# Row fetches by SyncE and ScalarE in place of one indirect gather in 64 and in 32, in a graph network kernel

## The chip, the cores and the metric

The kernel runs on one core of a Trainium2 chip. The metric is the device time of one execution in microseconds (us), the median over several runs. The engines are TensorE (PE, with its weight loads PEld), VectorE (DVE), ScalarE (ACT), GpSimd (POOL) and SyncE (SP), which only issues transfers. A name with q (SPq, ACTq) is the queue of the engine: issues of transfers, register instructions, waits.

## The reference

Four graph layers one after the other on 12,500 nodes of 64 features and 212,500 edges: a graph convolution, a hyperbolic layer, an attention network of three layers, and a relational network of two. The change touches the attention and the second relational layer:

```python
h = (x @ W).reshape(N, H, C)                          # 8 heads of 8
e = leaky_relu(alpha_s[src] + alpha_d[dst], 0.2)      # one logit for each edge and head
m = segment_max(e, dst);  ex = exp(e - m[dst])
out = segment_sum(h[src] * ex / denom[dst], dst)      # three times
# relational layer, twice
seg = dst * R + edge_type                              # R = 65 kinds of edges
mean = segment_sum(x[src], seg) / max(cnt, 1)
out = einsum('nrd,rdk->nk', mean, W_r) + x @ W_root + b
```

What costs most is `h[src]`: for each edge a row of 72 floats (64 features and 8 logit parts) is fetched from a table in DRAM by its node, and in the relational layers a row of 64 floats by node and kind.

## The kernel before

The edges, sorted by target, are cut into tiles of 128, one edge on each partition. Eight tiles (K = 8) are a chunk, and there are 208 chunks (1,664 tiles). An attention layer (`edges_attention`, once for each of three) and a relational layer (`edges_relational`, twice; the second is the last stage of the program, called the last loop here) pass over the 208 chunks once, with all engines in a software pipeline. What an engine does for chunk c stands in a list of steps with a lead: `(messages, 1)` does in turn t the work of chunk t + 1. `rounds` writes the list out for four turns and puts that in a hardware loop, so that buffers of four slots have fixed numbers q; `slotted` does the same with a second list of steps that runs every other turn.

The steps that matter here, with the lines of the profile:

- POOL, L2166 and L3027: for a chunk it waits until slot q of `from_src` is free (`filled` of the chunk four before) and until its row numbers are there (`gather_at`), then issues eight indirect gathers, one for each tile:

```python
def gather(c, q, i):
    pool.wait_ge(filled, free4(c))
    pool.wait_ge(gather_at, ready(c))
    for k in range(K):
        nc.gpsimd.indirect_dma_start(from_src[:, q, k, :], None, g.gat_src[:, :],
            bass.IndirectOffsetOnAxis(ap=src_at[:, q, k:k + 1], axis=0)).then_inc(got[q], 16)
```

- SP in attention: `load_rows` (L2155, lead 4) loads the places of the targets in their window, 256 KB, into one of two buffers once VectorE (`turned`, L2248) and ScalarE (`far_off`, L2212) have read that of two chunks before; `load_masks` (L2146, lead 3) loads two mask rows. In the last loop SP issues nothing until the end.
- DVE in attention: the two scans over 1,024 edges (L2291, L2298), `turned_ones` (L2248, lead 3), `logits` (L2270, lead 2), the first to read a gathered chunk, `messages` (L2281, lead 1), the last to read it and the one that raises `filled`, and eight adds into the sums (L2329). In the last loop: `messages` (L3152), the membership matrix (L3108), eight adds (L3169).
- ACT in attention: `targets` (L2183, lead 6) makes the row numbers for POOL. In the last loop: `fields` (L3042, L3044, lead 4), which waits for `filled` of the chunk four before, and `activate` (L3052), every other turn, whose result TensorE reads a turn later.
- `bases` (L183) loads numbers from SBUF into registers of an engine, up to eight at a time.
- `typed_tables` stands between the third attention layer and the first relational layer. Its TensorE begins with a wait for three weight loads (`pe.wait_ge(w_in, 48)`), then transposes the sums of the attention block by block (L2417), and only later multiplies with these weights (L2916).

## Time and profile before

| | |
|---|---|
| median of 3 runs | 17307.61 us (17297.01 to 17308.78) |
| profiled execution, its own time | 17330.74 us |
| its span | 17329.0 us |
| busy in it: PE, PEld | 12031.7 us, 8971.5 us |
| DVE, ACT, POOL | 12499.8 us, 7380.6 us, 11519.1 us |
| chain that ended last, largest share | POOL in the last loop (L3027), 8% |

Busy time of POOL counts only the part of a gather that the profile shows as running; the step from one gather to the next is longer. No engine is busy through the span, because its stages have different limits; so each stage is read by itself.

### The profile page before, as it was taken

Reading aid. Unit: us, or ns where it says so; the run is one execution under the profiler, and the core shown is the slowest. Engines: PE = TensorE matmul, PEld = TensorE weight load, DVE = VectorE, ACT = ScalarE, POOL = GpSimd, SP = SyncE. Lnnn points to the kernel's source line nnn. Section 1 sums busy time; section 2 is a strip of 40 time slices with the busy share of each in tenths; the row PEclk is TensorE's granted clock in tenths of the full one; section 3 lists DMA queues with packets and bytes.
Section 4 is the critical chain, followed back from the end, with each engine's and each line's share of the span. In section 5 each row is a group of like instructions: output and inputs, shape, how many; then the busy total and the mean of one; then the engine's idle time right before and its main releaser. Section 6 shows DMA issues by size and latency. Waiting matters only on the chain. (4 is left out here: it accounts for less than half of the span.)

```text
span 17329.0 us, 347894 instructions
## 1 busy us (share of the span) xinstructions
PE 12031.7 (69%) x77017; PEld 8971.5 (52%) x77018; DVE 12499.8 (72%) x30848; ACT 7380.6 (43%) x19204; POOL 11519.1 (66%) x11855
## 2 busy tenths in 40 slices
PE   4443338599997577777777777777777888844444
PEld 2222225466665466665666666666546565533333
DVE  7777769777777788887888878888766666634443
ACT  1111129555554566665666656666441222300000
POOL 2777750377775577776777767777307777777777
PEclk7555555677776555555556555655696777755555
DMA  6333344333335222223222232222494666511111
GB/s 235 96 93 94 93 93 123 109 102 103 102 102 90 73 58 58 58 58 73 58 58 58 58 78 58 58 58 58 161 381 126 180 185 178 176 45 26 26 26 32
DMA packets 1329349, 1689.67 MB, mean 98 GB/s; under 512 B 835210, under 2 KB 903562, under 8 KB 1296591
## 3 DMA queue, kind: packets, MB, share of 16 engines
q1 hardware_dynamic: 899089, 875.57, 17.4%
q0 software_dynamic: 412640, 597.16, 15.7%
q10 hardware_dynamic: 17474, 215.22, 3.3%
q8 instruction: 65, 1.06, 0.0%
q14 instruction: 81, 0.66, 0.0%
HBM read 1072.24 MB, written 618.81 MB: 98 GB/s over the span
## 5 line engine op out<-in xcount | busy, mean ns | idle before, releaser
L2166 POOL DMA_INDIRECT gat_from_src<-gat_src_dram,gat_src_at x4992 | 4821.8, 966 | 1680.6 <-issue 1520.8
L3213 PE MATMUL rel_ps_sum<-all_node,rel_msg 128*64 128x128 f32 x6656 | 1413.5, 383 | 1501.4 <-DVEq L3172 1471.3
L3027 POOL DMA_INDIRECT rel_from_src<-typed_dram,rel_src_at x1664 | 1651.1, 992 | 1079.7 <-ACT rel_src_at L3042 596.7
L2387 PE MATMUL gat_ps_sum<-all_node,gat_msg 128*80 128x128 f32 x9984 | 2266.1, 420 | 42.3 <-DVE gat_msg L2281 7.9
L3213 PEld LDWEIGHTS rel_ps_sum<-all_node,rel_msg 128*64 128x64 f32 x6656 | 1133.8, 199 | 1979.2 <-DVEq L3172 1230.3
L1630 POOL DMA_INDIRECT all_node<-hyp_dst_dram,hyp_src_at x1768 | 1724.9, 976 | 603.0 <-issue 513.3
L2387 PEld LDWEIGHTS gat_ps_sum<-all_node,gat_msg 128*80 128x80 f32 x9984 | 2057.5, 252 | 102.3 <-issue 42.7
L3027 POOL DMA_INDIRECT rel_from_src<-typed_next_dram,rel_src_at x1664 | 1593.3, 958 | 566.2 <-issue 493.0
L1094 POOL DMA_INDIRECT bucket_dram<-all_node,order_index x1664 | 1616.0, 971 | 524.3 <-issue 505.8
L2329 DVE TENSOR_TENSOR again_sums_x<-again_sums_x,gat_ps_sum 80x128 f32 x4992 | 1393.1, 279 | 385.4 <-DVE again_sums_x L2329 213.0
L2291 DVE TENSOR_TENSOR_SCAN gat_ps_log<-gat_masks,gat_top,gat_ps_log 8x1024 f32<-8x1024 bf16 x624 | 1461.9, 2343 | 228.3 <-DVE again_sums_x L2329 220.4
L2365 PE MATMUL gat_ps_log<-all_ident,gat_leaky 128*8 128x128 f32 x4992 | 1074.5, 388 | 710.5 <-DVE gat_leaky L2276 710.5
L2198 ACT ACTIVATE gat_off<-all_iota,gat_edge 128x128 bf16<-128x128 bf16 x4992 | 1515.8, 386 | 0.1
L3169 DVE TENSOR_TENSOR again_sums_x<-again_sums_x,rel_ps_sum 64x128 f32 x3328 | 908.5, 273 | 761.8 <-issue 355.8
L2298 DVE TENSOR_TENSOR_SCAN gat_top<-gat_masks,gat_ps_log 8x1024 f32<-8x1024 bf16 x624 | 1419.4, 2275 | 35.0
L2356 PE MATMUL gat_ps_dst<-gats_gat_here,gat_memberT 128*128 x9984 | 1130.1, 197 | 56.4 <-ACT gat_memberT L2218 43.8
L2356 PEld LDWEIGHTS gat_ps_dst<-gats_gat_here,gat_memberT 128*128 128x128 bf16 x9984 | 970.4, 108 | 344.7 <-issue 102.1
L1242 PE MATMUL order_ps_dst<-all_node 128*128 128x64 bf16 x4992 | 300.6, 240 | 1214.0 <-ACT all_node L1121 1156.2
L2228 ACT ACTIVATE gat_shift<-gat_shift 8x1 f32<-8x1 f32 x624 | 126.3, 202 | 2361.2 <-DVE gat_shift L2305 2361.2
L2365 PEld LDWEIGHTS gat_ps_log<-all_ident,gat_leaky 128*8 128x8 f32 x4992 | 510.0, 112 | 1027.9 <-DVE gat_leaky L2276 642.2
L2374 PE MATMUL gat_ps_top<-all_ident,gat_top 8*128 8x8 f32 x4992 | 501.7, 224 | 628.5 <-DVE gat_shift L2305 628.4
L1242 PEld LDWEIGHTS order_ps_dst<-all_node 128*128 128x128 bf16 x4992 | 271.6, 129 | 1258.9 <-issue 920.4
(571 smaller groups left out, 26929.1 us busy)
## 6 DMA issues: line engine op xcount, KB each, us to landing
typed_dram<-typed_res SPq DMA_DIRECT2D x98, 2080.0 KB, 7.2
typed_next_dram<-rel_res ACTq DMA_DIRECT2D x98, 2080.0 KB
gat_relrow<-in_rows_dram SPq DMA_DIRECT2D x624, 256.0 KB
all_node<-gcn_table_dram SPq DMA_DIRECT2D x1664, 48.0 KB
gat_from_src<-gat_src_dram,gat_src_at POOLq DMA_INDIRECT x4992
bucket_dram<-by_dst_zero POOLq DMA_DIRECT2D x48, 1326.0 KB, 6.6
gsum_rec<-bucket_dram SPq DMA_DIRECT2D x221, 288.0 KB, 2.8
all_node<-lo_rows_dram SPq DMA_DIRECT2D x221, 256.0 KB
```

Source lines behind the costliest of these rows:

```text
L1094: nc.gpsimd.indirect_dma_start(g.bucket[:, :], bass.IndirectOffsetOnAxis(ap=index[:, q, k:k + 1], axis=0), rec[:, q, k, :], None).then_inc ...
L1630: nc.gpsimd.indirect_dma_start(from_dst[:, q, k, :], None, g.hyp_dst[:, :], bass.IndirectOffsetOnAxis(ap=src_at[:, q, k:k + 1], axis=0)).t ...
L2166: nc.gpsimd.indirect_dma_start(from_src[:, q, k, :], None, g.gat_src[:, :], bass.IndirectOffsetOnAxis(ap=src_at[:, q, k:k + 1], axis=0)).t ...
L2198: last = nc.scalar.activation(off[:, k, :], g.iota16[:, :], ACT.Abs, scale=-1.0, bias=edge[:, q, REL, k:k + 1])
L2291: v.tensor_tensor_scan(log_flat, masks[:, q, 0, :], log_flat, top[:, 1 - q % 2, CE - 1:CE], ALU.add, ALU.max).then_inc(step_b, 1)
L2298: v.tensor_tensor_scan(top[:, q % 2, ::-1], masks[:, q, 1, ::-1], log_flat[:, ::-1], -BIG, ALU.add, ALU.max).then_inc(step_b, 1)
L2329: v.tensor_tensor(window, window, ps_sum[0:rows, k, :], ALU.add).then_inc(step_c, 1)
L2356: last = nc.tensor.matmul(dst_v[:, k, :], memberT[:, q % 2, w, k, :], own[:, w, :, :].rearrange("p n h -> p (n h)"), start=w == 0, stop=w ...
L2365: last = nc.tensor.transpose(ps_log[0:H, k, :], leaky[:, q % 2, k, :], g.ident[:, :])
L2387: last = nc.tensor.matmul(ps_sum[0:rows, k, :], msg[:, q % 2, k, :], member[:, q, k, :], start=True, stop=True)
L3027: nc.gpsimd.indirect_dma_start(from_src[:, q, k, :], None, table[:, :], bass.IndirectOffsetOnAxis(ap=src_at[:, q, k:k + 1], axis=0)).then_ ...
L3213: last = nc.tensor.matmul(ps_sum[0:D, k, :], msg[:, q % 2, k, :], member[:, q, k, :], start=True, stop=True)
```

## The change

One tile of a group is no longer gathered by POOL: in attention the last tile of every eighth chunk (one in 64), in the last loop the last tile of every fourth chunk (one in 32). Its 128 rows are fetched one by one into a side buffer `side`, each by a transfer of its own whose address is in a register, 16 rows in each turn, and one further transfer (`relay`) copies the side buffer to the slot when that is free. In attention SP issues all 128; in the last loop SP and ACT issue 64 each. The next group's rows wait until the side buffer has been copied. To give each turn of eight its own place, attention runs in a new loop `eights`. The two mask rows of a chunk are loaded by one transfer instead of two. The numbers of the rows are put on one partition when a stage begins (`single`); in the last loop VectorE turns them into integers first (`single_c`), and ScalarE and SyncE wait for that. In `typed_tables` the wait for the weights moves behind the transposes. The core of the diff:

```diff
+PIECE = 16
+GROUP = P // PIECE
+def fetch_piece(nc, eng, engine, rows, table, index, c, at, landed, top):
+    regs = bases(nc, engine, index, c, count=PIECE, per=PIECE, top=top)
+    for e, reg in enumerate(regs):
+        eng.dma_start(rows[at + e:at + e + 1, :], table[ds(reg, 1), :]).then_inc(landed, 16)
...
 # edges_attention, sync
+                sp.dma_start(single[:, :].rearrange("o (c e) -> o c e", e=P), g.src_p[...]).then_inc(single_in, 16)
+                sp.wait_ge(single_in, 16)
+                def relay(c, r, i):
+                    if r == GROUP - 1:
+                        for h in range(2):
+                            sp.wait_ge(side_in[h], 16 * (P // 2) * (i + 1))
+                            alone(sp, mark_s)
+                        sp.wait_ge(filled, free4(c))
+                        alone(sp, mark_s)
+                        sp.dma_start(from_src[:, r % 4, K - 1, :], side[:, :]).then_inc(side_out, 16)
+                def fetch(c, r, i):
+                    if r == 0 and not (isinstance(i, int) and i == 0):
+                        sp.wait_ge(side_out, 16 * i)
+                        alone(sp, mark_s)
+                    fetch_piece(nc, sp, ENG.SP, side, g.gat_src, single, c, r * PIECE, side_in[r // 4], N)
-                    for n, m in enumerate((g.first_mask, g.last_mask)):
-                        sp.dma_start(masks[:, q, n, :], m[ds(c * CE, CE)].partition_broadcast(H)
-                                     ).then_inc(mask_in[q], 16)
+                    sp.dma_start(masks[:, q, :, :], g.masks[:, ds(c * CE, CE)].partition_broadcast(H)).then_inc(mask_in[q], 16)
-                rounds(sp, [(load_rows, 4), (load_masks, 3)])
+                eights(sp, [(load_rows, 4), (load_masks, 3), (relay, 4), (fetch, 5)])
 # edges_attention, gpsimd
-                    for k in range(K):
+                    for k in range(K if r < GROUP - 1 else K - 1):
 # edges_attention, vector
+                    if r == GROUP - 1:
+                        dve.wait_ge(side_out, 16 * (i + 1))
...
 # typed_tables, tensor
-                pe.wait_ge(w_in, 48)
...
                 pe.wait_ge(flips.row_kept, FLIPS)
+                pe.wait_ge(w_in, 48)
...
 # edges_relational, second layer only
+                    for h in range(2):
+                        sp.dma_start(single[h]..., g.tile_rows[:, h * D:(h + 1) * D]...).then_inc(single_in, 16)
                     sp.dma_start(x[:, :, :], g.xs[:, :, :]).then_inc(x_in, 16)
+                    sp.wait_ge(single_c, 2)
+                    rounds(sp, [(relay, 4), (fetch(sp, ENG.SP, 0, mark_s), 5)])
-                    for k in range(K):
+                    for k in range(K if first or q < 3 else K - 1):
-                    slotted(act, [(fields, 4), (activate, None, LAG)])
+                    act.wait_ge(single_c, 2)
+                    slotted(act, [(fields, 4), (fetch(act, ENG.Activation, 1, mark_a), 5), (activate, None, LAG)])
+                    dve.wait_ge(single_in, 32)
+                    for h in range(2):
+                        v.tensor_copy(single[h], single[h].bitcast(F32)).then_inc(single_c, 1)
```

On SP in attention, in the middle of the loop, a turn was three transfers before (the places of the targets, and the two masks):

```order
L2155 ISA
L2155 DMA gat_relrow<-in_rows_dram 128x1024
L2146 DMA gat_masks<-first_mask_dram 8x1024
L2146 DMA gat_masks<-last_mask_dram 8x1024
```

Now the turn with the copy of the side buffer reads as follows, and the last two rows here come 16 times in this and in every other turn (ISA is the address in a register, TENSOR_LOAD the 16 row numbers):

```order
L2218 ISA
L2218 DMA gat_relrow<-in_rows_dram 128x1024
L2209 DMA gat_shared<-masks_dram 8x2x1024
L2192 ISA
L2196 DMA gat_from_src<-gat_side 128x72
L2201 REGISTER_ALU
L210 ISA
L210 TENSOR_LOAD gat_shared
L220 ISA
L220 DMA gat_side<-gat_src_dram 1x72
```

The fetches stand behind the two loads of the next turns, so SP comes to these only when 16 rows have been issued; its loop body goes from 22 such rows to 309, and VectorE's from 180 to 346 (it holds eight turns now).

On ACT in the last loop, in the middle, a turn was the row numbers for POOL, the fields of the edges, and every other turn the activation:

```order
L3040 REGISTER_ALU
L3042 ISA
L3042 ACTIVATE rel_src_at<-again_edges 128x8
L3044 ACTIVATE rel_edge<-again_edges 128x32
L3049 REGISTER_ALU
L3052 ACTIVATE rel_act_x<-rel_ps_node,rel_bias_col 128x128
```

Now it ends the turn before with its last row fetches and the activation, before it comes to the numbers of the next chunk:

```order
L220 ISA
L220 DMA rel_side<-typed_next_dram 1x64
L3147 REGISTER_ALU
L3150 ACTIVATE rel_act_x<-rel_ps_node,rel_bias_col 128x128
L3138 REGISTER_ALU
L3140 ISA
L3140 ACTIVATE rel_src_at<-again_edges 128x8
L3142 ACTIVATE rel_edge<-again_edges 128x32
```

The activation stands behind 16 row fetches of its turn, and the row numbers for POOL behind both.

## Rows read from the trace of the kernel before

**Rows 1.** The page, part 5, costliest groups: busy, mean ns, idle before

```profile
L2166 POOL DMA_INDIRECT gat_from_src<-gat_src_dram,gat_src_at x4992 | 4821.8, 966 | 1680.6 <-issue 1520.8
L3027 POOL DMA_INDIRECT rel_from_src<-typed_next_dram,rel_src_at x1664 | 1593.3, 958 | 566.2 <-issue 493.0
```

**Rows 2.** Timeline of POOL (start, us, idle before): first and last gather of two stages

```profile
5779.27 0.96 POOL L2166 DMA_INDIRECT gat_from_src<-gat_src_dram,gat_src_at  x1 [50.30 <-ACT gat_src_at L2183]
...
7890.28 0.95 POOL L2166 DMA_INDIRECT gat_from_src<-gat_src_dram,gat_src_at  x1 [0.30 <-issue]
...
15196.69 0.95 POOL L3027 DMA_INDIRECT rel_from_src<-typed_next_dram,rel_src_at  x1 [59.25 <-ACT rel_src_at L3042]
...
17296.03 0.95 POOL L3027 DMA_INDIRECT rel_from_src<-typed_next_dram,rel_src_at  x1 [0.30 <-issue]
```

**Rows 3.** Waits of the whole span: total us, times, longest

```profile
DVE gat_leaky L2270 <- DMA gat_from_src<-gat_src_dram,gat_src_at: 316.4, 470, 4.5
```

**Rows 4.** Timeline inside the second attention layer, one turn of SP and VectorE

```profile
9000.76 0.36 SPq L2155 DMA_DIRECT2D gat_relrow<-in_rows_dram  x1
9001.31 0.28 SPq L2146 DMA_DIRECT2D gat_masks<-first_mask_dram  x1
...
9008.72 0.49 DVE L2248 TENSOR_SCALAR gat_memberT<-gat_relrow,all_lane 128x1024 bf16<-128x1024 bf16 x1
...
9010.41 0.36 SPq L2155 DMA_DIRECT2D gat_relrow<-in_rows_dram  x1
```

**Rows 5.** Lines by themselves: instructions of a queue, ns min/median/max

```profile
L876 SPq DMA_DIRECT2D rel_prime<-in_L_gnn_bias x2: 248/254/260, 12973.4 to 12973.7; - x2
L2146 SPq DMA_DIRECT2D gat_masks<-first_mask_dram x624: 276/282/303, 5778.7 to 12300.6; - x156
L3007 SPq DMA_DIRECT2D rel_table_in<-counted_dram x1664: 332/333/1440, 12987.3 to 15116.4; - x185
L2779 SPq DMA_DIRECT2D typed_dram<-typed_res x98: 319/320/1693, 12422.4 to 12965.2; - x98
L3077 ACTq DMA_DIRECT2D typed_next_dram<-rel_res x98: 338/374/390, 13223.4 to 15186.1; - x98
L183 SPq TENSOR_LOAD <-again_base x208: 521/527/2516, 12986.4 to 15112.1; - x104
L183 ACTq TENSOR_LOAD <-all_order_at x196: 272/278/833, 13187.8 to 15185.7; - x196
```

**Rows 6.** Timeline of SP's queue in the first relational layer: eight window loads

```profile
14019.25 3.95 SPq L3007 DMA_DIRECT2D rel_table_in<-counted_dram  x8
```

**Rows 7.** Transfers by line: count, KB each, median us from issue to landing

```profile
gat_kept_dram<-gat_in_res SPq DMA_DIRECT2D x75, 160.0 KB, 2.1
typed_tab<-gat_kept_dram SPq DMA_DIRECT2D x5, 800.0 KB, 8.9
```

**Rows 8.** Timeline at the start of an attention layer

```profile
5777.73 0.86 SPq L2155 DMA_DIRECT2D gat_relrow<-in_rows_dram  x2
...
5801.67 0.69 DVE L2281 TENSOR_TENSOR gat_msg<-gat_from_src,gat_msg 128x512 f32<-128x512 f32 x1 [0.19 <-ACT gat_msg L2224]
```

**Rows 9.** Queue and ACT at the start of the last loop; integer cast on VectorE

```profile
15195.49 0.60 SPq L2994 DMA_DIRECT2D rel_bias_col<-in_L_gnn_res_b  x1
15195.65 0.21 ACT L3042 ACTIVATE rel_src_at<-again_edges 128x8 int32<-128x8 f32 x1 [9.73 <-DVEq L3185]
...
L362 DVE CAST prep_raw<-prep_raw x5: 1026/1027/1028, 64.7 to 69.0; 128x1664 f32<-128x1664 int32 x5
```

**Rows 10.** Timeline at the start of typed_tables

```profile
12363.52 0.35 SPq L2761 DMA_DIRECT2D typed_tab<-gat_kept_dram  x1
...
12382.29 13.59 PE L2417 MATMUL typed_bank<-all_ident,again_sums_x 80*128 80x80 f32 x100 [20.25 <-DMA typed_w<-in_L_gnn_W]
...
12385.80 0.33 DVE L2468 TENSOR_TENSOR typed_ad_own<-typed_tab 128x160 f32<-128x160 f32 x1 [23.44 <-ACT all_node L2425]
```

**Rows 11.** The page, part 3: queues that bring instructions, packets, MB

```profile
q8 instruction: 65, 1.06, 0.0%
q14 instruction: 81, 0.66, 0.0%
```

More of the change, by code:

```diff
@@ L146, in rounds, with eights, turn, in_fours @@
         turn(t, t // 4, t % 4)
+def eights(eng, steps, count=CHUNKS):
+    def turn(t, i, r):
+        for step, lead in steps:
+            if not isinstance(t, int) or 0 <= t + lead < count:
+                step(t + lead, (r + lead) % GROUP, i + (r + lead) // GROUP)
+    for t in range(-max(lead for _, lead in steps), 0):
+        turn(t, t // GROUP, t % GROUP)
+    full = (count - max(lead for _, lead in steps)) // GROUP
+    with eng.Fori(0, full) as i:
+        for r in range(GROUP):
+            turn(i * GROUP + r, i, r)
+    for t in range(GROUP * full, count):
+        turn(t, t // GROUP, t % GROUP)
+def in_fours(*steps):
+    def four(step):
+        return lambda c, r, i: step(c, r % 4, i * (GROUP // 4) + r // 4)
+    return [(four(step), lead) for step, lead in steps]
 def slotted(eng, steps, count=CHUNKS, slots=OWN_TILES):
@@ L328, in _ @@
                 sp.wait_ge(stored, 1)
-                for n, m in enumerate((g.first_mask, g.last_mask)):
+                for n in range(2):
+                    m = g.masks[n]
                     sp.dma_start(m[0:EP].rearrange("(g p e) -> p g e", p=P, e=P), mask[:, n, :, :]).then_inc(loaded, 16)
@@ L2113, in edges_attention @@
         mark_s = ph.sem("mark_s")
-        mask_in, got, rel_in = ([ph.sem(f"{n}{q}") for q in range(4)] for n in ("mask_in", "got", "rel_in"))
+        single_in, side_out = ph.sems("single_in side_out")
+        side_in = ph.sems("side_in0 side_in1")
+        mask_in, rel_in = ([ph.sem(f"{n}{q}") for q in range(4)] for n in ("mask_in", "rel_in"))
+        got = [ph.sem(f"got{r}") for r in range(GROUP)]
         rows = D + 2 * H
@@ L2118, in edges_attention @@
         lane2 = ph.sb("lane2", [P, 1])
-        masks = ph.sb("masks", [H, 4, 2, CE], BF16)
+        shared = ph.sb("shared", [D, 4, 2, CE], BF16)
+        masks = shared[0:H]
+        single = shared[D // 2:D // 2 + 1].rearrange("p q n e -> p (q n e)").bitcast(I32)[:, 0:CHUNKS * PIECE]
+        side = ph.sb("side", [P, D + H])
         from_src = ph.sb("from_src", [P, 4, K, D + H])
@@ L2333, in add @@
                     return step
[L2334 to L2337 removed]
+                eights(dve, [*in_fours((maxima_so_far, 1), (windows, 0), (maxima, 1), (rescale, 0), (shift_by, 1),
+                                       (turned_ones, 3), (add(0), 0), (of_targets, 2), (add(1), 0)),
+                             (logits, 2),
+                             *in_fours((add(2), 0), (leaky_logits, 2), (arguments, 1), (add(3), 0), (add(4), 0), (add(5), 0),
+                                       (tops_of, 1), (messages, 1), (add(6), 0), (add(7), 0))])
             @block.tensor
@@ L2976, in edges_relational @@
         else:
-            out_made, out_kept, stored, x_in = ph.sems("out_made out_kept stored x_in")
+            out_made, out_kept, stored, x_in, single_in, single_c, side_out = ph.sems(
+                "out_made out_kept stored x_in single_in single_c side_out")
+            side_in = [ph.sems(f"side_in{h}0 side_in{h}1") for h in range(2)]
+            halves = ph.sb("halves", [D, CHUNKS // 4 * D], I32)
+            single = [halves[D // 2 * h:D // 2 * h + 1, :] for h in range(2)]
+            side = ph.sb("side", [P, D])
+            top_row = OWN_TILES * P * R - 1
             x = ph.sb("x", [P, NT, D])
@@ L2980, in edges_relational, with fetch, step @@
             full, rest = N // P, N % P
+        def fetch(eng, engine, h, mark):
+            def step(c, q, i):
+                if q == 0 and not (isinstance(i, int) and i == 0):
+                    eng.wait_ge(side_out, 16 * i)
+                    alone(eng, mark)
+                fetch_piece(nc, eng, engine, side, table, single[h], c, h * D + q * PIECE, side_in[h][q // 2], top_row)
+            return step
         def place_of(engine, j, order, top):
@@ L3149, in messages @@
                 def messages(c, q, i):
-                    dve.wait_ge(got[q], 16 * K * (i + 1))
+                    dve.wait_ge(got[q], 16 * (K if first or q < 3 else K - 1) * (i + 1))
+                    if not first and q == 3:
+                        dve.wait_ge(side_out, 16 * (i + 1))
                     dve.wait_ge(summed, half_ready(c, 1) - 4)
```

41 lines of the change are left out of this document (27 added, 14 removed).

## The prediction

> **What bounds the kernel now.** I read the page's costliest groups first. Two lines on POOL hold 6,656 gathers of nearly one length, 966 and 958 ns, and the idle time ahead of them is almost all "issue", that is, POOL waits for nobody [rows 1]. Then POOL's timeline at both ends of a stage. In an attention layer the first gather starts at 5779.27 and the last of 1,664 at 7890.28, so a step is 2111.01 / 1663 = 1.2694 us; in the last loop it is (17296.03 − 15196.69) / 1663 = 1.2624 us [rows 2]. Once started POOL sets the pace of both. The waits say it from the other side: VectorE waited 316.4 us for gathered rows, 0.51 us for each of the 3 × 208 chunks [rows 3]. A chunk takes POOL 8 × 1.2694 = 10.16 us, so VectorE needs at most 9.65 of its own. With a gather in 64 gone the mean chunk is 63/8 × 1.2694 = 10.00 us: POOL stays ahead of VectorE as the bound, with 0.35 us of room. SP, in the same loop, starts a turn at 9000.76 and the next at 9010.41, and between them issues two more transfers by 9001.59 [rows 4]: over 8 us of each turn are free.
>
> **What is removed.** In attention 3 × 26 = 78 gathers, 78 × 1.2694 = 99.0 us. In the last loop 52, 52 × 1.2624 = 65.6 us. In the stage of the tables, TensorE's first transposes started at 12382.29 with a wait that ended on a weight load, and VectorE's first work on the table at 12385.80 behind them; the table itself, issued at 12363.52 for 0.35 [rows 10], lands some 8.9 us later [rows 7], at 12372.8. If only the kept rows and the table are waited for, the chain starts 10 to 13 us earlier; I take 13 less a little, −12.
>
> **What a row fetch costs its queue.** This decides the change. No row of before shows a queue issuing 16 transfers of one run of 256 bytes. Eight window loads took 3.95 us for eight issues of 0.333, so (3.95 − 0.333)/7 = 0.517 from one to the next, 0.184 of it around the issue (address, bookkeeping) [rows 5, 6]. The issue grows with the number of runs: 0.254 for a single small one, 0.282 for 8 mask rows, 0.333 for 128 rows [rows 5]. So a fetch costs x between 0.254 + 0.184 = 0.438 and 0.517; 0.282 + 0.184 = 0.466 is for eight runs, and one run is nearest to the low end. I take 0.45 on SP. ACT's queue is slower for one shape (338 at least against 320, median 374) [rows 5], so 0.018 to 0.054 more: 0.456 to 0.50, taken 0.465. The 16 row numbers come by one register load: 521 to 527 ns for eight against 272 to 278 for one [rows 5] is 36 ns a register, so 0.527 + 8 × 0.036 = 0.81, with what surrounds it about 1.0.
>
> The Trainium skill ("Runtime: NRT & Kernel Launch", section on instruction fetch mechanics) says that a register load costs about 200 ns a register even in bulk. That would be 3.2 us for 16. The 36 ns of this trace speak against it, and the sum does not use it.
>
> **SP in attention.** Per turn: the two loads with their waits 1.15, the fetches 1.0 + 16x. Per eight turns, 8 × 2.15 + 128x, plus the copy of the side buffer: issue 0.35, landing of the last row and of the copy, about 2.1 each by the nearest transfer [rows 7], less what turns over in between, 3.4 with the loop branch. Hence 20.8 to 21.3 + 128x, against POOL's 63 × 1.2694 = 79.97 us. At x = 0.438 it is 77.4, at 0.45 it is 78.9, at 0.459 it is 80, at 0.517 87.5. The gain exists only while SP keeps up. At the start of a layer SP also has to load `single` and to issue 16 fetches before each load of targets' places: in before both went out at 5777.73 and the first messages came at 5801.67 [rows 8], 24 us later. I count 11 us more for VectorE there; POOL, four chunks ahead, needs its first slot back after about 42 us, which leaves 42 − 24 − 11 = 7 us unused. SP must then make good what it lags at 79.97 − 78.9 = 1.1 us per group, 26 times, and does. The forecast for attention is −99 with little lost.
>
> **The last loop.** SP issued nothing there. Its chain for a group of four turns is 8.4 + 64x = 37.2 against POOL's 31 × 1.2624 = 39.13: it fits. ACT's holds the same 64 fetches, and between them the three activations, the wait for the last landing, SP's copy and its landing, because the next rows wait for the copy: 10.1 + 64x. At 0.456 that is 39.3, at 0.465 39.9, at 0.50 42.1. ACT is so the tighter one, and from x = 0.454 sets the pace: 51 groups × (39.9 − 39.13) is 37, less the 11 us that POOL's four slots give once, 26 lost. At the start, ACT made the first row numbers at 15195.65, straight behind VectorE's numbers [rows 9]. Now it first waits for `single_c`: two loads (0.6 each [rows 9] and 2.1 to land [rows 7]), two integer casts of 3,328 numbers, 1027/1664 = 0.617 ns a number [rows 9], 2.05 us each; and SP's and ACT's lead turn with 16 fetches, 8.4, stands before the second. That is 3.3 + 4.1 + 8.4 = 16 to 18, taken 17. The last loop: −65.6 + 17 + 26 = −23; with an ACT chain that just fits, −49.
>
> **Sum.** −99 − 12 − 23 = −134, made against the profiled 17330.74 us, which lies 23 us (0.13%) over the median 17307.61. From the median that is 17174; I put 17180 for small losses at the two kinds of start.
>
> **The rivals.**
> (a) Both queues fit, with nothing lost (x at most 0.455 on both): −99 − 12 − 49 = −160, 17148. For it: the one-run issue of 0.254. Against it: ACT's slower issues.
> (b) ACT only is late: −134, or between −140 and −50 as x on ACT runs from 0.46 to 0.49 (51 × (10.1 + 64 × 0.49 − 39.13) − 11 = 107 lost). This is the forecast.
> (c) The other side: SP's queue becomes the bound of attention. VectorE's `turned_ones` waits for places of targets whose load stands behind 16 fetches, `filled` comes late, and POOL stands. The loss of a layer is 26 × (G − 79.97) + 11 − 7, G = 21.3 + 128x: at x = 0.466 (G = 80.9) 28 us, three layers 84, and with the ACT chain at 0.49 the whole change is −99 − 12 − 65.6 + 17 + 107 + 84, or +31; at 0.48 on SP a layer loses 75 and the change is +170. It decides from about x = 0.466, which is the issue time of a transfer of eight runs and well inside my bounds.
> (d) The longer loops no longer stay in the engine's instruction store. SP's body goes from 22 listed rows to 309, VectorE's from 180 to 346, and in before the queues that bring instructions moved only 65 and 81 packets in 17 ms [rows 11], that is, the loops of before ran without fetching again. If each pass of eight turns now stops for 1.5 us, a wait like the landing of a small transfer, SP's G rises to 80.4 and VectorE loses 0.2 us a turn of its 0.35: 0 to 15 us a layer, total −135 to −90, near (b); with several stops a pass on both engines, 4 us, SP's G is 83 and a layer loses 80: total +105.
> The Trainium skill (same page and section) gives the store as 512 instructions for most engines and says that a branch outside its window stops the engine until the page is fetched. The 309 rows, with the moves between them, are near that size; no stretch of before shows such a stop.
> (e) The register load costs far more than 36 ns a register: at 200, SP has 8 × 2.4 us more a group, G = 98, and the change costs 26 × 18 × 3 = 1,400 us less 99. One row speaks against it and none for it.
>
> **How the numbers follow.** (a) 0.27, (b) with the mild form of (d) 0.37, (c) with the hard form of (d) 0.33, (e) 0.03. About 0.2%, 35 us, is what a measurement of this kernel can tell from no change. Of (c), which begins at zero net gain in attention, a third lies still below −35 and a quarter inside ±35; so faster 0.27 + 0.34 + 0.03 = 0.64, same 0.11, slower 0.25. The likeliest case by itself is 17140 to 17255. The range reaches from 17135, where all goes well, up to 17420, which takes in (c) to x = 0.475 or so, and leaves some 2 in 10 out.
>
> **What the profile after will show.** If right: first to last gather 2111 → about 2080 in each attention layer, VectorE's wait for gathered rows down but not gone, SP's queue nearly full with steps of 0.45 from one row to the next, a register load of about 0.8; in the last loop POOL's first gather unchanged to 8 us later, its span about 2060, with waits of VectorE for the side buffer or of POOL for ACT's row numbers, and TensorE's transposes of the tables some 12 us nearer to the stage's start. (c) shows as VectorE waiting for `gat_relrow`, and POOL idle behind it; (d) as instruction packets in the hundreds and gaps at the loop's end on SP or VectorE. The prediction is wrong if a fetch step is over 0.466 on SP, or if 16-row turns make SP late for the first chunks by more than the 7 us counted.

## The result

| | before | after |
|---|---|---|
| median of 5 runs | 17306.08 us (17296.0 to 17308.78) | 17213.9 us (17208.51 to 17228.21) |
| profiled execution, its span | 17329.0 us | 17206.8 us |

The changed kernel is 0.5% faster: ratio 0.9949, 95% interval 0.9937 to 0.9961, 92 us less. The forecast was 17180 in a range of 17135 to 17420. The two profiled spans differ by 122 us; some 30 of them belong to these two executions, since that of before lies 25 us over its median and that of after 5 below. So the stages are compared in the traces, and the sizes of the whole in the medians.

POOL's timeline after, its first and last gather of the three attention layers and of the last loop (columns as in [rows 2], which they answer to):

```profile
5776.98 0.96 POOL L2230 DMA_INDIRECT gat_from_src<-gat_src_dram,gat_src_at  x1 [50.29 <-ACT gat_src_at L2247]
7854.97 0.95 POOL L2230 DMA_INDIRECT gat_from_src<-gat_src_dram,gat_src_at  x1 [0.30 <-issue]
7966.90 0.96 POOL L2230 DMA_INDIRECT gat_from_src<-gat_src_dram,gat_src_at  x1 [54.78 <-ACT gat_src_at L2247]
10075.16 0.95 POOL L2230 DMA_INDIRECT gat_from_src<-gat_src_dram,gat_src_at  x1 [0.30 <-issue]
10189.57 0.96 POOL L2230 DMA_INDIRECT gat_from_src<-gat_src_dram,gat_src_at  x1 [55.18 <-ACT gat_src_at L2247]
12291.25 0.95 POOL L2230 DMA_INDIRECT gat_from_src<-gat_src_dram,gat_src_at  x1 [0.30 <-issue]
12925.34 0.96 POOL L3125 DMA_INDIRECT rel_from_src<-typed_dram,rel_src_at  x1 [565.47 <-ACT rel_src_at L3140]
15146.09 0.95 POOL L3125 DMA_INDIRECT rel_from_src<-typed_next_dram,rel_src_at  x1 [68.59 <-ACT rel_src_at L3140]
17173.57 0.95 POOL L3125 DMA_INDIRECT rel_from_src<-typed_next_dram,rel_src_at  x1 [0.31 <-issue]
```

The same of before, as far as [rows 2] does not have them:

```profile
7993.80 0.96 POOL L2166 DMA_INDIRECT gat_from_src<-gat_src_dram,gat_src_at  x1 [54.37 <-ACT gat_src_at L2183]
10105.80 0.95 POOL L2166 DMA_INDIRECT gat_from_src<-gat_src_dram,gat_src_at  x1 [0.30 <-issue]
10210.62 0.96 POOL L2166 DMA_INDIRECT gat_from_src<-gat_src_dram,gat_src_at  x1 [55.16 <-ACT gat_src_at L2183]
12976.57 0.96 POOL L3027 DMA_INDIRECT rel_from_src<-typed_dram,rel_src_at  x1 [569.86 <-ACT rel_src_at L3042]
```

The stage of the tables begins with SP's first load of its table, at 12363.52 before [rows 10]; after it is

```profile
12335.92 0.35 SPq L2829 DMA_DIRECT2D typed_tab<-gat_kept_dram  x1
```

From one first gather to the next, with what lies between two stages, the first layer went from 2214.5 to 2189.9 us (−25), the second from 2216.8 to 2222.7 (+6), the third up to the stage of the tables from 2152.9 to 2146.4 (−7), that stage from 613.0 to 589.4 (−24), the first relational layer, which the change does not touch, from 2220.1 to 2220.8 (+1), the last loop to the end of the span from 2132.3 to 2060.7 (−72). The three attention layers so gained 26 us, where 99 were forecast. The first layer's gathers took 2078.0 us, just 26 steps less than 2111.0; the second's took 2108.3, hardly less than its 2112.0 before. Something else than POOL's gathers bounds the second layer and the third.

The waits after, whole span (total us, times, longest):

```profile
POOL gat_from_src L2230 <- DVE gat_msg L2348: 98.1, 151, 2.0
DVE gat_ps_log L2358 <- issue: 242.8, 82, 3.7
DVE gat_memberT L2312 <- DMA gat_relrow<-in_rows_dram: 185.9, 89, 20.3
```

VectorE's wait for gathered rows, 316.4 us before [rows 3], is gone from the list. In its place VectorE waits for the places of the targets, which SP loads, and POOL now waits for VectorE.

SP's queue in the second layer, around the end of a pass of eight turns (start, us, x count):

```profile
8984.04 2.29 SPq L220 DMA_DIRECT2D gat_side<-gat_src_dram  x6
8989.43 0.37 SPq L2218 DMA_DIRECT2D gat_relrow<-in_rows_dram  x1
8991.22 0.29 SPq L2209 DMA_DIRECT2D gat_shared<-masks_dram  x1
8993.03 6.45 SPq L220 DMA_DIRECT2D gat_side<-gat_src_dram  x16
8999.88 0.36 SPq L2218 DMA_DIRECT2D gat_relrow<-in_rows_dram  x1
9000.43 0.29 SPq L2209 DMA_DIRECT2D gat_shared<-masks_dram  x1
...
9070.55 0.37 SPq L2218 DMA_DIRECT2D gat_relrow<-in_rows_dram  x1
9072.57 0.29 SPq L2209 DMA_DIRECT2D gat_shared<-masks_dram  x1
```

Three things are to be seen. Sixteen fetches take 6.45 us, a step of (6.45 − 0.23)/15 = 0.415. Behind the last fetch of a turn in mid-pass the next load comes after 8999.88 − 8999.48 = 0.40 us; behind the last fetch of a pass it comes after 8989.43 − 8986.33 = 3.10. And from that load to the masks it is 1.8 and 2.0 us there, against 0.55 in the next turn. SP's waits for other engines that stand there take 0.02 us each, since what they wait for has come before, and 2.5 of the 3.10 us lie directly behind the branch instruction. This pass of SP is 9070.55 − 8989.43 = 81.1 us (the median of the layer, from branch to branch, is 81.4), POOL's 63 steps are 80.0, and SP never waited for another engine in the layer, only for its own transfers: SP's queue is the bound. VectorE has the same at the restart of its own loop; here its first scan in mid-pass and at a restart:

```profile
8998.90 2.34 DVE L2358 TENSOR_TENSOR_SCAN gat_ps_log<-gat_shared,gat_top,gat_ps_log 8x1024 f32<-8x1024 bf16 x1 [0.23 <-DVE again_sums_x L2396]
...
9060.69 2.34 DVE L2358 TENSOR_TENSOR_SCAN gat_ps_log<-gat_shared,gat_top,gat_ps_log 8x1024 f32<-8x1024 bf16 x1 [3.49 <-issue]
```

SP's shorter gaps have a pattern. Counted in the trace, they come every 128 instructions, in the changed kernel as in e9 below, and take 0.34 to 0.40 us. The first of a pass stands 103 instructions behind the branch in the first layer, 8 in the second and 38 in the third. The one that stands 8 behind takes more, 1.1 us here and 1.3 in the median. It is most of the stop ahead of the masks, and the second layer's pass is the longest of the three (80.1, 81.4 and 80.9 us in the median).

The page's queues that bring instructions, which answer to [rows 11]: q14 went from 81 packets to 890.

```profile
q14 instruction: 890, 7.29, 0.1%
q8 instruction: 65, 1.06, 0.0%
```

Lines by themselves, which answer to [rows 5] (ns min/median/max):

```profile
L220 SPq DMA_DIRECT2D gat_side<-gat_src_dram x9984: 224/228/332, 5778.7 to 12288.2; - x200
L220 ACTq DMA_DIRECT2D rel_side<-typed_next_dram x3328: 227/235/552, 15138.5 to 17138.2; - x196
L210 SPq TENSOR_LOAD <-gat_shared x624: 1132/1147/1307, 5777.3 to 12280.6; - x156
```

The theory that I took from this: SP's own work of a pass is some 77 us and fits under POOL's 80.0, as forecast; a body of 482 instructions (counted in the trace between two branches back) has to be fetched again in each pass, and the stops for that, 2.5 us at the restart and 1.1 to 2.4 in the middle, carry it over. The rivals: VectorE's own restart stop is the bound, or the fetches as such are too much work.

### The profile page after: what moved, and what is told of

It reads as the page before. It is cut to its first block and busy times, and to the rows that moved or that the text cites. A ratio compares the mean times of both kernels' runs of the same rounds, so it can differ in the third digit from the quotient of the medians.

```text
span 17206.8 us, 398106 instructions
## 1 busy us (share of the span) xinstructions
PE 12023.1 (70%) x77017; PEld 8979.5 (52%) x77018; DVE 12471.9 (72%) x30850; ACT 7302.4 (42%) x19204; POOL 11362.2 (66%) x11725
## 3 DMA queue, kind: packets, MB, share of 16 engines
q14 instruction: 890, 7.29, 0.1%
## 5 line engine op out<-in xcount | busy, mean ns | idle before, releaser
L2230 POOL DMA_INDIRECT gat_from_src<-gat_src_dram,gat_src_at x4914 | 4733.0, 963 | 1718.0 <-issue 1459.8
L3125 POOL DMA_INDIRECT rel_from_src<-typed_next_dram,rel_src_at x1612 | 1536.8, 953 | 560.2 <-issue 484.0
L2358 DVE TENSOR_TENSOR_SCAN gat_ps_log<-gat_shared,gat_top,gat_ps_log 8x1024 f32<-8x1024 bf16 x624 | 1461.9, 2343 | 372.0 <-issue 242.8
L2365 DVE TENSOR_TENSOR_SCAN gat_top<-gat_shared,gat_ps_log 8x1024 f32<-8x1024 bf16 x624 | 1419.2, 2274 | 28.0
L2433 PE MATMUL gat_ps_log<-all_ident,gat_leaky 128*8 128x128 f32 x4992 | 1004.8, 369 | 486.8 <-DVE gat_leaky L2343 486.1
L2442 PEld LDWEIGHTS gat_ps_top<-all_ident,gat_top 8*128 8x128 f32 x4992 | 468.5, 176 | 978.2 <-issue 978.2
```

Of the source, the lines that this page charges most:

```text
L2358: v.tensor_tensor_scan(log_flat, masks[:, q, 0, :], log_flat, top[:, 1 - q % 2, CE - 1:CE], ALU.add, ALU.max).then_inc(step_b, 1)
L2365: v.tensor_tensor_scan(top[:, q % 2, ::-1], masks[:, q, 1, ::-1], log_flat[:, ::-1], -BIG, ALU.add, ALU.max).then_inc(step_b, 1)
L2433: last = nc.tensor.transpose(ps_log[0:H, k, :], leaky[:, q % 2, k, :], g.ident[:, :])
L3125: nc.gpsimd.indirect_dma_start(from_src[:, q, k, :], None, table[:, :], bass.IndirectOffsetOnAxis(ap=src_at[:, q, k:k + 1], axis=0)).then_ ...
```

## The experiments

**The parts alone.** e1 keeps the change of attention, e2 that of the last loop, e6 that of the tables' stage; all else is as before.

> The change in attention alone (row fetches by SP, one mask transfer, loops of eight turns); the stage of the tables and the last loop as before. Theory: the layers themselves gave back most of the 99 us, because SP's queue is the bound of the second and third layer (81.3 us for a pass of eight turns against POOL's 80.0). From the trace of the changed kernel, first gather to first gather, the three layers changed by -25, +6 and -20, so -35 to -42 us, ratio 0.9976 to 0.9980. Rival, the one of the prediction: near -99, ratio 0.9943, with the loss somewhere else in the program.

Measured: 17310.81 us against 17321.53, ratio 0.9991 (0.9982 to 1.0), −11 us. Less than my expectation of −35 to −42, and a tenth of the forecast's −99. The interval leaves it at 0 to −31. My expectation had counted the third layer at −20; by the rows above it is −7, so the traces say −26, which the interval holds. The first two layers took 17 us more in e1's trace than in the changed kernel's: SP's passes are longer there by 0.3 and 0.5 us (80.4 and 81.9 in the median). Why its stops differ between the two programs stays open. The rival, −99 with the loss elsewhere, is out: the loss is in attention.

> The change in the last loop alone. Theory: both queues fit, POOL stays the bound, and the start costs some 9 us: -65.6 - 6 + 9, so -55 to -65 us, ratio 0.9962 to 0.9968. Rival (ACT's chain sets the pace, as forecast): -23 to -49 us with spans of POOL over 39.5 us for a group of 31 gathers.

Measured: 17273.0 against 17321.53, ratio 0.997 (0.9958 to 0.9982), −48 us. By the time alone that is in the rival's range, and the interval, −31 to −73, holds the theory's too; the trace tells them apart. In the changed kernel's trace SP copies its side buffer once in four turns. Its first copies, while the queues run ahead of POOL, and two later ones:

```profile
15243.77 0.49 SPq L3109 DMA_DIRECT2D rel_from_src<-rel_side  x1
15280.39 0.48 SPq L3109 DMA_DIRECT2D rel_from_src<-rel_side  x1
15317.41 0.48 SPq L3109 DMA_DIRECT2D rel_from_src<-rel_side  x1
...
16086.37 0.48 SPq L3109 DMA_DIRECT2D rel_from_src<-rel_side  x1
16125.58 0.48 SPq L3109 DMA_DIRECT2D rel_from_src<-rel_side  x1
```

The chain of both queues takes 36.6 to 37.0 us by itself and is later held at POOL's 39. ACT's activations begin only at 15335.71, behind these first three copies, but they change nothing: the next copies, at 15353.53, 15389.99, 15426.35 and 15462.73, are 36.4 us apart. The chain fits. What is lost is the start: POOL's first gather of the loop comes 15146.09 − 15076.55 = 69.5 us behind the last gather of the loop before it (rows further down), against 15196.69 [rows 2] − 15136.49 = 60.2 before. One pair of traces says little here, since this gap varies with nothing changed at it. e3 leaves the last loop as it was and has 48.8:

```profile
15150.72 0.95 POOL L3053 DMA_INDIRECT rel_from_src<-typed_dram,rel_src_at  x1 [0.30 <-issue]
15199.52 0.95 POOL L3053 DMA_INDIRECT rel_from_src<-typed_next_dram,rel_src_at  x1 [47.85 <-ACT rel_src_at L3068]
```

Over all traces the gap is 48.8 to 60.2 us in the four without the change of the last loop (before, e1, e3, e6; mean 54.8) and 67.9 to 76.0 in the six that have it as made (the changed kernel, e2, e4, e5, e7, e9; mean 71.5). The start costs some 17 us, and the gathers of the loop take 67 less, 2094.7 us in the mean of the four and 2027.6 in that of the six: −50 together, which e2's time bears out.

> Only the wait for the weights in the stage of the tables moves behind the transposes. The prediction's step: -12 us, since TensorE's first transpose starts 10.4 us earlier behind the stage's start in the changed kernel; ratio 0.9993. Rival (more is behind it, because last gather of attention to first gather of the relational layer went from 661 us with attention changed alone to 634): -20 to -27 us, ratio 0.9985 to 0.9988. Third: 0, the stage's stores to the table are its bound.

```diff
-                pe.wait_ge(w_in, 48)
...
                 pe.wait_ge(flips.row_kept, FLIPS)
+                pe.wait_ge(w_in, 48)
```

Measured: 17294.37 against 17312.33, ratio 0.999 (0.9981 to 0.9999), −18 us, between −12 and the rival's −20 to −27; its interval, −2 to −33, holds all of these. The parts alone add up to −11 − 48 − 18 = −77, against −92 for the whole, a difference that their intervals hold too. TensorE's timeline of e6, its first transposes:

```profile
12363.19 7.84 PE L2417 MATMUL typed_bank<-all_ident,again_sums_x 80*128 80x80 f32 x64 [1.53 <-PEq L213]
12371.29 5.06 PE L2417 MATMUL typed_bank<-all_ident,again_sums_x 80*128 80x80 f32 x36 [0.25 <-ACT all_node L2425]
```

They begin at 12363.19 instead of 12382.29 [rows 10], 19.1 us earlier, with the start of the stage less than 1 us apart in the two traces: they wait neither for weights nor for the table.

**The length of the loop alone.** e3 is the kernel before with `eights` in place of `rounds` on SP, POOL and VectorE in attention, for example:

```diff
-                rounds(sp, [(load_rows, 4), (load_masks, 3)])
+                eights(sp, in_fours((load_rows, 4), (load_masks, 3)))
```

> The kernel before with loops of eight turns instead of four on SP, POOL and VectorE in attention, and nothing else. SP's body stays near 36 instructions, VectorE's goes from 208 to about 410. Theory (instruction store): VectorE stops 2.6 to 3.0 us at every restart of its loop, SP and POOL do not; VectorE's own turn rises from 9.65 to about 9.97 us, which is still under POOL's 10.16, so the time is that of before within 10 us and VectorE's waits for gathered rows fall from 316 us to about 120. Rival (VectorE's stall alone is what bounds attention in the changed kernel, at 81.3 us a pass): VectorE's waits for gathered rows fall to under 40 us. Second rival (the stall comes from something else than the length of the loop): no stall, waits near 316.

Measured: 17327.03 against 17321.53, ratio 1.0003 (0.9994 to 1.0012): the same. VectorE's body is 405 instructions instead of 208 and stops at every restart, SP's has 91 and does not. The waits of e3:

```profile
DVE gat_ps_log L2317 <- issue: 243.9, 72, 3.5
DVE gat_leaky L2296 <- DMA gat_from_src<-gat_src_dram,gat_src_at: 185.4, 262, 4.5
```

The idle time at a stop is 243.9/72 = 3.4 us and comes from the length alone; it costs nothing that the time shows (the interval is −10 to +21 us) while VectorE has its 0.5 us a turn. Its waits for gathered rows fell from 316 to 185 us, not to 120, so it has more room left than I thought, and at a pass of 80 us it is not the bound. The packets of q14 went from 81 to 452.

**SP with less to do.** e4 fetches rows at fixed addresses:

```diff
-                    fetch_piece(nc, sp, ENG.SP, side, g.gat_src, single, c, r * PIECE, side_in[r // 4], N)
+                    bases(nc, ENG.SP, single, c, count=PIECE, per=PIECE, top=N)
+                    for e in range(PIECE):
+                        row = r * PIECE + e
+                        sp.dma_start(side[row:row + 1, :], g.gat_src[row * 97:row * 97 + 1, :]).then_inc(side_in[r // 4], 16)
...
```

> The changed kernel, but in attention SP fetches rows at addresses fixed in the program instead of the rows that the numbers name (the features of one tile in 64 are so not those of the reference). A fetch is one instruction instead of three, and seven loads of one register in a turn give SP the time back that this saves; so SP has about the same work in a turn, and a body of some 300 instructions instead of 482. Theory (SP bound by the work plus fetches of instructions): the stop at the restart of SP's loop (2.5 us) and those in its middle (0.3 to 1.3) are gone, a pass is POOL's 80.0 us or VectorE's 79.4, and the three layers take 30 to 45 us less than in the changed kernel: 17170 to 17185, ratio 0.9921 to 0.9930. Rivals: SP is bound by the work of the fetches as such, or VectorE's own stall is the bound: no change against the changed kernel, ratio 0.9945 to 0.9952, pass 81.3.

Measured: 17148.87 against 17321.53, ratio 0.9899 (0.9884 to 0.9914), −173 us, past my expectation, and for a reason that spoils the test: its trace holds none of the register loads of the attention layers. Nothing used what they loaded, and so, it seems, they were left out of the program. SP had not the same work but 30 us a pass less, with a body of 212 instructions. What it still shows: VectorE's body is the same 405 instructions with the same stops, and the layers run at 80.0 us a pass. This ends the rival that VectorE's stop is the bound. It says nothing on whether SP's work or its instruction fetches are.

e7 takes one of SP's transfers away instead and leaves its body long (443 instructions): ACT's queue loads the places of the targets.

```diff
+                def load_rows(c, q, i):
+                    act.wait_ge(turned, free2(c))
...
-                eights(sp, [(load_rows, 4), (load_masks, 3), (relay, 4), (fetch, 5)])
+                eights(sp, [(load_masks, 3), (relay, 4), (fetch, 5)])
...
-                rounds(act, [(exponents, 1), (targets, 6), (distances, 2), (fields, 4), (zero_ones, 2), (exp_shift, 2),
+                rounds(act, [(load_rows, 4), (exponents, 1), (targets, 6), (distances, 2), (fields, 4), (zero_ones, 2), (exp_shift, 2),
```

> The changed kernel, but in attention ACT's queue issues the load of the targets' places (256 KB a turn) at the start of its turn, so SP has masks, fetches and the copy. Bodies stay long: SP some 410 instructions, VectorE 405. Theory: SP's pass falls from 81.4 to some 77 us, instruction stops included, and what SP is late with no longer holds VectorE; VectorE at 77 + 2.8 is just inside POOL's 80.0, so the layers are POOL's again: 40 to 75 us less than the changed kernel, 17140 to 17175 by 17306 before, ratio 0.9905 to 0.9925. Rival (VectorE's restart stall bounds the layers): no change against the changed kernel, 0.9945 to 0.9952. Second rival: ACT, which waits 3.8 us a turn for VectorE, becomes late with its far ones, slower than the changed kernel.

Measured: 17140.99 against 17312.33, ratio 0.9903 (0.9888 to 0.9919), −171 us, at the upper end of the gain that the theory gave. POOL's first and last gather of the second layer in e7:

```profile
7970.59 0.96 POOL L2223 DMA_INDIRECT gat_from_src<-gat_src_dram,gat_src_at  x1 [54.73 <-ACT gat_src_at L2247]
10041.94 0.95 POOL L2223 DMA_INDIRECT gat_from_src<-gat_src_dram,gat_src_at  x1 [0.30 <-issue]
```

2071.4 us for 1,638 gathers instead of 2108.3. Both stops at a restart are still there (2.6 us on SP, 2.8 on VectorE in the median), so a stop costs only where its engine has no room.

**The same instructions, fewer restarts.** This is the test of the cause. e9 writes four passes into the body of SP's loop, so that the order and the number of instructions that run stay the same (1,922 in the loop for four passes, against 4 × 482 = 1,928) and one restart in four is left:

```diff
-                eights(sp, [(load_rows, 4), (load_masks, 3), (relay, 4), (fetch, 5)])
+                eights(sp, [(load_rows, 4), (load_masks, 3), (relay, 4), (fetch, 5)], passes=4)
```

> The changed kernel, but SP's loop in attention holds four passes (32 turns, some 1,930 instructions) instead of one: the same instructions in the same order, and a restart only in every fourth pass. Theory (the stop at the restart belongs to the branch back, 2.4 us more than a restart of a short loop): SP's pass falls by 3/4 x 2.4 = 1.8 us where it is the bound, from 81.4 to about 79.6 in the second layer and from 81.0 to 79.2 in the third, so POOL takes over at 80.0: 1.4 + 1.0 us a pass, 25 passes each, 55 to 65 us with the shorter tails less than the changed kernel at best, at least 30; ratio 0.991 to 0.993. Rival 1 (fetching the code itself costs, wherever it is needed: the stops in the middle of the body, 0.3 to 1.3 us, come as often or grow): the pass stays at 81 us or more, ratio 0.9945 or higher. Rival 2 (SP bound by the work of its fetches): no change either, with the stop at the restart gone.

Measured: 17157.06 against 17316.57, ratio 0.9909 (0.9892 to 0.9925), −160 us: 67 more than the change as it was made, with none of SP's work taken away, and the two intervals do not touch. The layers' gathers took 2078, 2076 and 2075 us, where the changed kernel had 2078, 2108 and 2102. SP's queue of e9 at a pass boundary inside the body, and at a restart:

```profile
8235.17 6.43 SPq L221 DMA_DIRECT2D gat_side<-gat_src_dram  x16
8242.05 0.36 SPq L2219 DMA_DIRECT2D gat_relrow<-in_rows_dram  x1
8242.68 0.29 SPq L2210 DMA_DIRECT2D gat_shared<-masks_dram  x1
...
8312.55 6.44 SPq L221 DMA_DIRECT2D gat_side<-gat_src_dram  x16
8322.38 0.37 SPq L2219 DMA_DIRECT2D gat_relrow<-in_rows_dram  x1
8323.04 0.28 SPq L2210 DMA_DIRECT2D gat_shared<-masks_dram  x1
```

0.45 us behind the last fetch without a branch, 3.39 with one. The page of e9 still counts 781 packets of q14, nearly as many as the 890. So fetching instructions in sequence costs some 0.35 us every 128 instructions, and the branch back costs 2.4 to 2.9. That the code is no longer there and is fetched again is the reading that the packets suggest; the test itself shows that the restart is what costs. Both rivals (the code costs wherever it is fetched; the fetches are too much work) would have left the time where it was.

**The same fetches in a short body.** e5 has groups of four turns: POOL gathers 64 rows of a tile, SP fetches the other 64, and every loop is short again (SP 246 instructions, VectorE 207).

```diff
-                        sp.dma_start(from_src[:, r % 4, K - 1, :], side[:, :]).then_inc(side_out, 16)
+                        sp.dma_start(from_src[D:P, r, K - 1, :], side[:, :]).then_inc(side_out, 16)
...
-                    for k in range(K if r < GROUP - 1 else K - 1):
+                    for k in range(K):
+                        n = D if q == 3 and k == K - 1 else P
...
-                            from_src[:, q, k, :], None, g.gat_src[:, :],
+                            from_src[0:n, q, k, :], None, g.gat_src[:, :],
...
```

> The changed kernel, but in attention a group is four turns: POOL gathers rows 0 to 63 of the last tile of every fourth chunk (a gather of 64 rows), SP fetches rows 64 to 127, 16 a turn as before, and copies them in one transfer every four turns. The rows that SP fetches are as many as in the changed kernel and its work of a turn is the same plus one more copy in eight turns (2.6 us), but its loop has some 245 instructions instead of 482, VectorE's 208 instead of 405. Theory (instruction store): no stop at a restart on either, SP's own work for eight turns 76.5 + 2.6 = 79 us, under 80. If a gather of 64 rows costs half of one of 128 the three layers are bound by POOL at 80.0 us for eight turns and the time is 17150 to 17175 by the 17306 of before, ratio 0.991 to 0.9925; if it costs as much as a full one, POOL is back at 81.3 and the ratio is 0.9955 to 0.9965. Rival (SP is bound by the work of its fetches, not by instruction fetch): SP is still the bound at 81 us or more for eight turns and never waits.

Measured: 17225.84 against 17312.33, ratio 0.9948 (0.9934 to 0.9961), −86 us. The packets of q14 are back at 108 and no restart of SP's or VectorE's loop stops for over 0.3 us. But the gather of 64 rows costs nearly what one of 128 does. In its timeline the last gather of the second layer, of 64 rows, and the first, of 128:

```profile
7989.40 0.96 POOL L2230 DMA_INDIRECT gat_from_src<-gat_src_dram,gat_src_at  x1 [54.40 <-ACT gat_src_at L2247]
10086.66 0.92 POOL L2230 DMA_INDIRECT gat_from_src<-gat_src_dram,gat_src_at  x1 [0.30 <-issue]
```

0.92 against 0.96 us, so next to nothing is taken off POOL: 32 gathers at 1.257 us from one to the next, the median step, are 40.2 us for four turns. SP copies its side buffer at 8794.90 and 8835.12:

```profile
8794.90 0.49 SPq L2196 DMA_DIRECT2D gat_from_src<-gat_side  x1
...
8835.12 0.49 SPq L2196 DMA_DIRECT2D gat_from_src<-gat_side  x1
```

40.2 us as well, with no wait for another engine in between, so POOL and SP are level and e5 does not tell which of them bounds. What it does show: eight turns with the work of the changed kernel and one copy more take SP 80.4 us in a short body, where the changed kernel takes 81.4 without that copy. A copy with its landing adds 2.8 (from the masks to the next fetch it is 4.6 us in such a turn and 1.8 in the others), so SP's own work for a pass is at most 77.6 us, under 80.0. That is the figure on which the forecast rested, and it holds. e5's time is lower than I expected for a gather of 64 rows at full cost (0.9955 to 0.9965): its layers took 2097, 2097 and 2103 us, and those of before, with as many gathers, 2111, 2112 and 2117. No run here says where these 14 us a layer come from.

**The start of the last loop.** e8 lets ACT make a chunk's numbers before it fetches rows.

```diff
-                if q == 0 and not (isinstance(i, int) and i == 0):
+                if q == 0 and isinstance(i, int) and i == 0:
+                    eng.wait_ge(single_c, 2)
+                elif q == 0:
                     eng.wait_ge(side_out, 16 * i)
...
-                    act.wait_ge(single_c, 2)
-                    slotted(act, [(fields, 4), (fetch(act, ENG.Activation, 1, mark_a), 5), (activate, None, LAG)])
+                    slotted(act, [(fields, 4), (fetch(act, ENG.Activation, 1, mark_a), 4), (activate, None, LAG)])
```

> The changed kernel, but in the last loop ACT makes the numbers of a chunk before it fetches rows (its fetch has lead 4 instead of 5 and stands behind the numbers), and waits for the integer row numbers only before its first fetch. Theory (the start of the last loop costs what ACT's first numbers wait for): POOL's first gather comes 10 to 16 us earlier behind the first relational layer, the rest stays: ratio 0.0006 to 0.0009 lower than that of the changed kernel, 0.9938 to 0.9943. Rival (SP's copy, which needs ACT's last landing, comes too late for VectorE with a lead of 4): a group goes over 39.1 us and the time rises by 20 us or more.

Measured: 17224.35 against 17312.33, ratio 0.9952 (0.9939 to 0.9966), no gain against 0.9949, though these intervals, some 23 us to either side, could not show one of 10. The trace has POOL's first gather 59 us behind the loop before it instead of 69.5, as expected, but the loop's gathers take 3.5 us more (2031.0). e10 puts e7 and e8 together:

> The two edits together that gave something alone: ACT's queue loads the targets' places in attention, and in the last loop ACT makes a chunk's numbers before it fetches rows. Theory: the effects add, 71 us less than the changed kernel by the first (17141 by 17312 before) and some 6 to 10 by the second, since POOL's first gather of the last loop came 10 us earlier in its trace: ratio 0.9895 to 0.9901. Rival: the second gives nothing in time (its median was that of the changed kernel): 0.9903.

Measured: 17137.45 against 17316.57, ratio 0.9898 (0.9882 to 0.9915), −179 us, the lowest median of all, with e7's inside its interval. In its trace the gap ahead of the last loop is the shortest of all that fetch rows there; the rows are e10's, then the last of the loop before and the first of the last loop in the changed kernel:

```profile
15014.60 0.95 POOL L3127 DMA_INDIRECT rel_from_src<-typed_dram,rel_src_at  x1 [0.30 <-issue]
15067.11 0.95 POOL L3127 DMA_INDIRECT rel_from_src<-typed_next_dram,rel_src_at  x1 [51.56 <-ACT rel_src_at L3142]
```

```profile
15076.55 0.95 POOL L3125 DMA_INDIRECT rel_from_src<-typed_dram,rel_src_at  x1 [0.30 <-issue]
```

52.5 us instead of 69.5. With e8's 59.2 the gap is back in the range of the kernels without row fetches in the last loop (48.8 to 60.2), so what the start costs is indeed what ACT's first numbers wait for. The loop's gathers take 2033.4 us here, against 2026.9 in e7. Whether the difference pays in time is not settled: 0.9898 and e7's 0.9903 have intervals that reach three times their difference to either side.

## Why the prediction came out as it did

The time fell in the range and the sign was right, 34 us above the forecast of 17180. The three terms did worse than their sum: attention gave 73 us less than forecast (−26 in the traces), the last loop 25 more and the tables 6 more by their own runs. That the sum came so near is in part luck.

**Attention, forecast −99 "with little lost".** That SP's queue decides was right, and its work was sized well in all but detail: a fetch costs 0.415 us, not 0.45 and not even within my 0.438 to 0.517, since the issue of one run is 0.228 and not 0.254; the load of 16 numbers takes 1.15 us instead of 0.81. The sum, 21.3 + 128x = 78.9, came out at some 77 (76.5 without any stop, at most 77.6 by e5). Its fixed part is 20.6 by the terms named beside it (8 × 2.15 + 3.4), not 20.8 to 21.3; by that the forecast would have been 78.2. The term that failed is that of the rival (d), which I gave its mild form, 1.5 us a pass on SP and 0 to 15 us a layer. SP stops 3.6 us in a pass of the first layer, 4.9 in the second and 4.0 in the third (the sum of its gaps of over 0.3 us that stand behind no wait), and the pass came to 80.1, 81.4 and 80.9. These are the stops of the hard form (4 us, G = 83, a loss of 80 us a layer). They cost so little only because SP's work was over 2 us less than I had it, and that too is luck. The first layer kept its gain; the other two gave most of theirs back, by passes and by an end of the layer at which VectorE is further behind POOL: −26 of −99 is left in the traces, −11 in e1. That e9 gives it back without touching the work shows this. VectorE's stop, which I had also counted at 0.2 us a turn, is 0.35 and costs nothing that e3 and e4 could show.

**The last loop, forecast −23.** The case (b), ACT's chain late by 26 us, did not happen. ACT's fetch costs 0.407 (16 in 6.34 us, less 0.235), not 0.465, and the chain 36.4 to 37.0 us with the activations, not 39.9. The start cost the 17 us that I gave it, and e2's −48 is the −49 of a chain that fits: in this stage the case (a) had it, term by term.

**The stage of the tables, forecast −12.** Measured −18, and −24 in the changed kernel's trace. The interval of e6 alone would allow the −12; the trace does not, since the transposes begin 19 us earlier. The term was mis-sized by the wait that I put last: I let the transposes begin with the landed table, but they read the attention's sums, which are there when the stage begins.

**The rest.** The slower rival (c) was right in where the price would show (VectorE behind `gat_relrow`, POOL behind VectorE) and wrong in its cause, which was the stops and not x. (e) is out: 16 numbers cost 1.15 us, 72 ns each. The Trainium skill ("Runtime: NRT & Kernel Launch", section on instruction fetch mechanics) has some 200 for a register; the page has register loads from HBM in view, and these load from SBUF, so its figure was not a price for this case, and the measurement decides. The same section's warning, that a taken branch outside the window stops for a fetch and that fetching in sequence is mostly hidden, agrees with e3 and e9, with 2.4 to 2.9 us for the one and 0.35 for the other. From its store of 512 instructions one must not conclude that a body of up to 512 restarts freely: here one of 405 stopped at each restart, one of 246 at none, and nothing in between was run.

## What to carry to other kernels

Before a loop body is doubled or many small issues are written into it, count its instructions on each engine: the price in these runs is a stop of some 2.5 us at every branch back of a body of 405 or more, and none up to 246. It is paid only where that engine has no room, so it belongs in the sum of the engine that is nearly full. If it is, take a transfer away from it to a queue that idles, or unroll further so that it branches back less often: four passes in the body were 67 us better here than one. Where a stage's time hangs on a single gap between two instructions, read the gap in every trace that has the same code before believing a pair: this one varied by 11 us with nothing changed. And where a sum hangs on hundredths of a microsecond a transfer, rows of other shapes don't price it: they missed the fetch on one side and the register load on the other.

## What the runs showed of the hardware

- A loop body of 405 instructions (VectorE) or of 443, 482 and 1,922 (SP) stops for 2.4 to 2.9 us, in the median of a layer, at each branch back; bodies of 64 to 246 instructions on SP, VectorE and ACT restart in 0.1 to 0.3 us. Between 246 and 405 nothing was run.
- Running forward in such a long body costs SP some 0.35 us every 128 instructions, and 1.3 to 1.5 in the median where that place stands 8 instructions behind the branch back. A packet of the queue that brings instructions has 8 KB (7.29 MB in 890 packets).
- An indirect gather of 64 rows on POOL takes 0.92 us against 0.95 to 0.96 for 128: half the rows save 4% of it.
- A transfer of one row whose address is in a register costs SP 0.415 us of its queue and ACT 0.407; a load of 16 registers 1.15 us, where 8 take 0.53.
